# Fewer, wider VectorE operations for the router's choice, the slot's place and the attention's division

## The reference

```
x = x + attn_a(norm(x))    # delta-rule recurrence, 16 heads of 8, state 8x8 per head, gate, Wout
x = x + ffn(norm(x))       # 8 experts, top 2, capacity 640, weights w_g, c_fc, c_proj
x = x + attn_b(norm(x))    # linear attention: q' (k'^T v) / (q' . sum k'), then W_out, b_out
x = x + ffn(norm(x))       # the same experts again
```

```
top_v, top_i = top_k(logits, 2)
exp_rank = cumsum(one_hot(top_i) in the order (choice, token)) - 1
keep = exp_rank < cap
exp_out = gelu(batch @ c_fc) @ c_proj
```

## Time and profile before

| | |
|---|---|
| median of 3 runs | 482.74 us (482.45 to 485.15) |
| the profiled execution | 483.11 us |
| its span, first to last instruction | 481.4 us |
| busy: PE, DVE, ACT, POOL | 87%, 64%, 49%, 53% |
| granted TensorE clock, mean | 0.951 |
| DVE instructions | 744 |

### The profile page before, as it was taken

The page is one execution under the profiler, slowest core; times in us unless marked ns, Lnnn a source line. Parts: engine busy times, 40 slices in busy tenths (PEclk is TensorE's granted clock), DMA queues, the critical chain, the costliest instruction groups (busy, mean ns, idle before and its releaser), DMA issues.

```text
span 481.4 us, 8149 instructions
## 1 busy us (share of the span) xinstructions
PE 418.6 (87%) x2850; PEld 304.6 (63%) x2850; DVE 310.0 (64%) x744; ACT 236.5 (49%) x371; POOL 257.0 (53%) x321
## 2 busy tenths in 40 slices
PE   7889795878898899999898999889878979999970
PEld 6534352334697899999864333345347969999960
DVE  4898789999663323415696999899985602431364
ACT  4877755343230354343168988878762204435320
POOL 4899584899678865465305000020556732556470
PEclk9999899787899999999999999999997999999995
DMA  5457580993171232225624434595011121221276
GB/s 143 128 154 291 157 259 27 321 311 109 36 231 50 67 89 61 82 61 206 185 63 104 99 96 99 136 284 186 24 33 46 51 84 40 63 87 58 81 253 203
DMA packets 50328, 60.89 MB, mean 126 GB/s; under 512 B 7152, under 2 KB 29296, under 8 KB 50288
## 3 DMA queue, kind: packets, MB, share of 16 engines
q1 hardware_dynamic: 42672, 47.50, 33.4%
q0 software_dynamic: 4608, 8.47, 5.4%
q10 hardware_dynamic: 3008, 4.40, 2.8%
HBM read 29.78 MB, written 25.31 MB: 114 GB/s over the span
## 4 chain that ended last, share of the span: by engine, by line
PE 38%; DVE 11%; issue 9%; ACT 8%; DMA 6%; POOL 5%; ACTq 1%; POOLq 0%; DVEq 0%; SPq 0%
PE ps L1412 34%; DVE feat L1332 5%; POOL slots_x L517 4%; ACT expo L865 3%; PE ps L1568 2%; DMA xe<-slots_x 2%; DMA last_got<-chosen_y 2%; ACT rows_x L712 1%; DMA chosen_y<-ye,y_to 1%; DMA slots_x<-rows_x,put_at 1%; ACT xnT L610 1%; DVE stats L1064 1%; POOL chosen_y L567 1%; DVE part L1312 1%; DVE xres L1359 1%
## 5 line engine op out<-in xcount | busy, mean ns | idle before, releaser
L567 POOL DMA_INDIRECT chosen_y<-ye,y_to x80 | 79.1, 989 | 67.8 <-DVE ye L1277 49.4
L1332 DVE SCALAR_TENSOR_TENSOR feat<-expo,ps 128x1024 f32<-128x1024 f32 x64 | 75.1, 1214 | 6.3 <-ACT expo L865 6.2
L751 ACT ACTIVATE hT<-ps 128x640 f32<-128x640 f32 x64 | 45.2, 706 | 69.1 <-PE ps L1412 69.1
L517 POOL DMA_INDIRECT slots_x<-rows_x,put_at x64 | 62.8, 980 | 28.8 <-issue 17.7
L865 ACT ACTIVATE expo<-ps,minus_one 128x1024 f32<-128x1024 f32 x64 | 69.9, 1115 | 11.7 <-PE ps L1412 9.6
L1412 PE MATMUL ps<-cproj_sb,hT 128*128 128x128 f32 x640 | 74.6, 275 | 0.3
L1416 PE MATMUL ps<-ident 128*128 128x128 f32 x546 | 68.0, 285 | 7.5 <-DMA slots_x<-rows_x,put_at 4.1
L1412 PEld LDWEIGHTS ps<-cproj_sb,hT 128*128 128x128 f32 x640 | 72.9, 192 | 0.6 <-ACT hT L751 0.6
L1416 PEld LDWEIGHTS ps<-ident 128*128 128x128 f32 x546 | 63.9, 147 | 10.0 <-DMA slots_x<-rows_x,put_at 5.1
L1227 DVE TENSOR_TENSOR xe_low<-ps,xeT 128x640 fp32r<-128x640 f32 x16 | 13.2, 825 | 86.3 <-ACT xeT L610 86.3
L500 POOL TENSOR_TENSOR read<-state,qT 128x512 f32<-128x512 f32 x30 | 38.1, 1276 | 15.1 <-DVE state L1013 14.9
(11 more groups left out here) (238 smaller groups left out, 702.1 us busy)
## 6 DMA issues: line engine op xcount, KB each, us to landing
chosen_y<-empty_rows SPq DMA_DIRECT2D x32, 256.0 KB
decay<-k_rows SPq DMA_DIRECT2D x30, 256.0 KB, 5.1
stk<-part SPq DMA_DIRECT2D x96, 64.0 KB, 2.0
slots_x<-empty_rows SPq DMA_DIRECT2D x16, 325.0 KB, 6.1
xe<-slots_x SPq DMA_DIRECT2D x16, 325.0 KB, 2.9
cfc_sb<-in_L_ffn_c_fc SPq DMA_DIRECT2D x2, 2048.0 KB, 9.8
got<-chosen_y SPq DMA_DIRECT2D x8, 256.0 KB, 5.8
got<-chosen_y ACTq DMA_DIRECT2D x8, 256.0 KB, 7.0
```

What stands on the lines that cost most here:

```text
L517: pool.indirect_dma_start(out=slots_x[k], out_offset=bass.IndirectOffsetOnAxis(ap=put_at[:, c, kk, t:t + 1], axis=0), in_=rows_x[:, kk * N ...
L567: pool.indirect_dma_start(out=chosen_y[k], out_offset=bass.IndirectOffsetOnAxis(ap=y_to[:, b, i:i + 1], axis=0), in_=ye[:, b, i * D:(i + 1 ...
L751: act.activation(hT[:, b, f, :].rearrange("p (a n) -> p a n", a=2), ps[:, 2 + 2 * (f % 2):4 + 2 * (f % 2), 0:HALF], ACT.Gelu).then_inc(h_r ...
L1332: dve.scalar_tensor_tensor(out=feat[:, g % 4, :], in0=expo[:, g % 3, :], scalar=1.0, in1=flat(ps[:, pair, :]), op0=ALU.min, op1=ALU.max).t ...
```

## The change

Four things are done. In `choose` the test for a tie is made once for all four tiles into a new tile `tie`, ahead of `hit`, and one subtraction takes back the marks. In `locate` one product takes the place of two; for that the ranks are laid out by expert and then tile (`e t` where it was `t e`), in `rank` on TensorE too, and the reduction reads `table` with the tile innermost in its result. In `divide` one product takes the place of two; `att` gets the order (tile, g, gp, a, d) of its columns, so the columns of W_out are loaded in that order, by two transfers in place of one.

```diff
+        tie = sb("tie", [P, TB])
-        table = sb("table", [P, 4, TB, NE])
+        table = sb("table", [P, 4, NE, TB])
-            att = sb("att", [P, 2, TB, D], F32, b)
+            att = sb("att", [P, 2, TB, 4, 2, 2, HD], F32, b)
...
-            sp.dma_start(wnat[:, 3, :], W_out).then_inc(wnat_in, 16)
+            for n in range(2):
+                sp.dma_start(wnat[:, 3, :].rearrange("p (g n r) -> p g n r", g=4, n=2)[:, :, n, :],
+                             W_out[:, n * D // 2:(n + 1) * D // 2].rearrange("p (g r) -> p g r", g=4)).then_inc(wnat_in, 16)
...
                 link(ins)
+                steps[0] += 1
+                dve.tensor_tensor(tie[:], eight[:, :, 0], eight[:, :, 1], ALU.is_equal).then_inc(route_step, 1)
                 dve.tensor_tensor(hit, lg.unsqueeze(2).broadcast_to((P, TB, 2, NE)),
                                   eight[:, :, 0:2].unsqueeze(3).broadcast_to((P, TB, 2, NE)),
                                   ALU.is_equal).then_inc(logit_used, 1)
                 dve.wait_ge(logit_used, k * NB + c + 1)
-                for t in range(TB):
-                    ins = dve.scalar_tensor_tensor(out=hit[:, t, 1, 0:1], in0=eight[:, t, 0:1], scalar=eight[:, t, 1:2],
-                                                   in1=hit[:, t, 1, 0:1], op0=ALU.is_equal, op1=ALU.subtract, reverse1=True)
-                link(ins)
+                dve.wait_ge(route_step, steps[0])
+                link(dve.tensor_tensor(hit[:, :, 1, 0], hit[:, :, 1, 0], tie[:], ALU.subtract))
...
-                for kk in range(2):
-                    ins = dve.tensor_tensor(
-                        table[:, 2 * kk:2 * kk + 2, :, :], ranks[:, 2 * kk:2 * kk + 2, :, :],
-                        chosen[:, c, kk, :, :].rearrange("p e t -> p t e").unsqueeze(1).broadcast_to((P, 2, TB, NE)),
-                        ALU.mult)
-                ins.then_inc(rank_used, 1)
+                dve.tensor_tensor(table[:].rearrange("p (k n) e t -> p k n (e t)", k=2),
+                                  ranks.rearrange("p (k n) e t -> p k n (e t)", k=2),
+                                  chosen[:, c, :, :, :].rearrange("p k e t -> p k (e t)").unsqueeze(2)
+                                  .broadcast_to((P, 2, 2, NE * TB)), ALU.mult).then_inc(rank_used, 1)
                 dve.wait_ge(rank_used, k * NB + c + 1)
-                link(dve.tensor_reduce(place, table[:], AX_X, ALU.add))
+                link(dve.tensor_reduce(place, table[:].rearrange("p r e t -> p r t e"), AX_X, ALU.add))
...
-                for a_ in range(2):
-                    ins = dve.tensor_tensor(
-                        att[:, c % 2, :, gp * 64:(gp + 1) * 64].rearrange("p t (g a d) -> p t g a d", a=2, d=HD)[:, :, :, a_, :],
-                        rows.rearrange("p (t g) r -> p t g r", g=4)[:, :, :, 9 * a_:9 * a_ + HD],
-                        rden[:, gp, :, a_].rearrange("p (t g) -> p t g", g=4).unsqueeze(3).broadcast_to((P, TB, 4, HD)),
-                        ALU.mult)
-                ins.then_inc(att_ready, 1)
+                dve.tensor_tensor(att[:, c % 2, :, :, gp, :, :].rearrange("p t g a d -> p (t g) a d"),
+                                  pairs[:, :, :, 0:HD],
+                                  rden[:, gp, :, :].unsqueeze(3).broadcast_to((P, TB * 4, 2, HD)),
+                                  ALU.mult).then_inc(att_ready, 1)
...
-                ch = chosen[:, c, :, :, :].rearrange("p k e t -> p k t e")
-                up = upto[:, c, :, :, :].rearrange("p k e t -> p k t e")
-                twice = lambda ap: ap.unsqueeze(1).broadcast_to((P, 2, TB, NE))
+                ch = chosen[:, c, :, :, :]
+                up = upto[:, c, :, :, :]
+                twice = lambda ap: ap.unsqueeze(1).broadcast_to((P, 2, NE, TB))
...
-                    pe.wait_ge(wnat_in, 32)
+                    pe.wait_ge(wnat_in, 48)
```

More of the change, by code:

```diff
@@ L1177, in _ @@
                 if b is not None:
-                    locate(0, b, ps[:, 5 if b < NB - 1 else 4, P:2 * P].rearrange("p (r t e) -> p r t e", r=4, e=NE),
+                    locate(0, b, ps[:, 5 if b < NB - 1 else 4, P:2 * P].rearrange("p (r e t) -> p r e t", r=4, e=NE),
                            ps[:, 5, 3 * P:3 * P + 4 * TB].rearrange("p (r t) -> p r t", r=4))
@@ L1373, in _ @@
                 dve.tensor_copy(kvl[:, :, a_, :, cols], heads[:, :, a_, :, cols]).then_inc(kvl_ready, 1)
-            ranks_in = lambda bank: ps[:, bank, P:2 * P].rearrange("p (r t e) -> p r t e", r=4, e=NE)
+            ranks_in = lambda bank: ps[:, bank, P:2 * P].rearrange("p (r e t) -> p r e t", r=4, e=NE)
             for n in range(2, N_SLOT):
@@ L1537, in rank @@
             def rank(k, c, bank):
-                out = ps[:, bank, P:2 * P].rearrange("p (r t e) -> p r t e", r=4, e=NE)
-                ch = chosen[:, c, :, :, :].rearrange("p k e t -> p k t e")
-                up = upto[:, c, :, :, :].rearrange("p k e t -> p k t e")
-                twice = lambda ap: ap.unsqueeze(1).broadcast_to((P, 2, TB, NE))
+                out = ps[:, bank, P:2 * P].rearrange("p (r e t) -> p r e t", r=4, e=NE)
+                ch = chosen[:, c, :, :, :]
+                up = upto[:, c, :, :, :]
+                twice = lambda ap: ap.unsqueeze(1).broadcast_to((P, 2, NE, TB))
                 if k == 0 or c:
                     pe.wait_ge(chosen_ready, k * NB + c + (k == 0 and c < NB - 1))
-                mm(out, ones_bf[:], base_share[:].unsqueeze(2).broadcast_to((P, 4, TB, NE)), stop=False)
+                mm(out, ones_bf[:], base_share[:].unsqueeze(3).broadcast_to((P, 4, NE, TB)), stop=False)
                 for b in range(c):
                     first, second = (upto[:, b, kk, :, TB - 1] for kk in range(2))
-                    mm(out[:, 0:3, :, :], ones_bf[:], first.unsqueeze(1).unsqueeze(2).broadcast_to((P, 3, TB, NE)),
+                    mm(out[:, 0:3, :, :], ones_bf[:], first.unsqueeze(1).unsqueeze(3).broadcast_to((P, 3, NE, TB)),
                        start=False, stop=False)
-                    mm(out[:, 2, :, :], ones_bf[:], second.unsqueeze(1).broadcast_to((P, TB, NE)), start=False, stop=False)
-                    mm(out[:, 3, :, :], minus_bf[:], second.unsqueeze(1).broadcast_to((P, TB, NE)), start=False, stop=False)
+                    mm(out[:, 2, :, :], ones_bf[:], second.unsqueeze(2).broadcast_to((P, NE, TB)), start=False, stop=False)
+                    mm(out[:, 3, :, :], minus_bf[:], second.unsqueeze(2).broadcast_to((P, NE, TB)), start=False, stop=False)
                 pe.wait_ge(chosen_ready, k * NB + c + 1)
@@ L1553, in rank @@
                 mm(out[:, 2, :, :], ones_bf[:], up[:, 1, :, :], start=False, stop=False)
-                mm(out[:, 2, :, :], ones_bf[:], up[:, 0, TB - 1:TB, :].broadcast_to((P, TB, NE)), start=False, stop=False)
+                mm(out[:, 2, :, :], ones_bf[:], up[:, 0, :, TB - 1:TB].broadcast_to((P, NE, TB)), start=False, stop=False)
                 mm(out[:, 3, :, :], minus_bf[:], up[:, 1, :, :], start=False, stop=False)
@@ L1848, in turn_att @@
                 for t in range(TB):
-                    ins = pe.transpose(ps[:, bank, t * P:(t + 1) * P], att[:, c % 2, t, :], ident[:])
+                    ins = pe.transpose(ps[:, bank, t * P:(t + 1) * P], att[:, c % 2, t, :, :, :, :].rearrange("p g n a d -> p (g n a d)"), ident[:])
                 ins.then_inc(att_turned, 1)
```

## The result

| | before | after |
|---|---|---|
| median, 20 runs each, on one chip | 483.70 us (480.67 to 488.05) | 486.99 us (483.84 to 490.42, one at 540.02) |
| ratio to before, 95% interval | | 1.0072 (1.0044 to 1.0099) |
| the profiled execution, its span | 483.11, 481.4 us | 489.33, 487.5 us |
| DVE instructions, busy | 744, 310.0 us | 712, 311.6 us |

The kernel became 3.5 us slower by the ratio (0.72%; the medians differ by 3.3) where I forecast 0.1. The execution of 540.02 us had a granted clock of 0.73 and is left out of the ratio. The kernel has 32 VectorE instructions less, and VectorE is busy for longer.

The account below looks back on a forecast made before the run. VectorE's chain of waits, through TensorE and ScalarE, was taken to bound two stages ahead of the experts. First stage +0.29 and second -0.21 give +0.08 us on the profiled 483.11; from the median 482.74, forecast 482.8 us, range 480.4 to 485.4.

Parts of the forecast that it names:

- What bounds the kernel, and where the edits stand: VectorE's chain of waits in two stages ahead of the experts; each edit priced where it stands, block 3 worth nothing.
- The tie test in the first call: Choices of blocks 0 and 1: test held by one GpSimd product, each about 0.1 us slower; block 2 worth nothing.
- through two GpSimd products: Rival, chance 0.08: first-call tie test held through two adjoining products, each choice 1.2 us behind, +2.4 us, 485.2 us.
- The counter-row: Clamp at line 972 (23.34 us) ended inside six GpSimd products, 0.14 us after the second; used against the double hold.
- The tie test in the second call: Blocks 0 and 1: 0.39 us saved per choice, but line 1359's projection is next late, so 0.05 us gained each.
- The place: Eight calls: one table product saves 0.065 us, the stepped reduction costs 0.09; net +0.03 us each, six on the path.
- The division and W_out's load: One product (0.425 us) for two (0.49): -0.065 us each, three on the chain, -0.2; the two loads stay hidden.
- The second stage as a whole: 300 to 390 us: choices -0.1, divisions -0.2, places +0.09, together -0.21 us.
- The clock: Rival, chance 0.09 either way: TensorE's low-clock stretch near 112 to 121 us ends at once (480.2) or lasts (486.3).

Follow-up runs that it names:

- experiment 11: Changed kernel with four GpSimd fills of 128x512 ahead of block 0's reading product; 488.47 us, ratio 1.0087 to the kernel before.
- 12: Changed kernel with three GpSimd fills ahead of block 0's reading product; 487.59 us, ratio 1.0097 to the kernel before.
- experiment 13: Changed kernel with the first three scatters of each block's row one to three slots later; 485.26 us, ratio 1.0034 to the kernel before.
- experiment 2: Kernel before with the new tie correction alone; 487.25 us, ratio 1.0077 to the kernel before.
- experiment 5: Changed kernel with one tie-test operand and the last scan's reset pattern in PSUM in the first call; 483.30 us, ratio 0.9958 to the kernel before.
- 4: Changed kernel with the tie test moved behind the comparison; 485.87 us, ratio 1.0073 to the kernel before.
- 7: Changed kernel with four more MAX8 ahead of the real ones in the first call; 488.40 us, ratio 1.0087 to the kernel before.
- 8: Changed kernel with two more MAX8 ahead of the real ones in the first call; 488.25 us, ratio 1.0069 to the kernel before.
- experiment 14: Changed kernel with a 128x64 GpSimd fill behind each of the first two scatters of block 0's row; 489.45 us (four executions), ratio 1.0102 to before.
- experiment 10: Changed kernel with GpSimd's scatter put between the reading and decay products of a slot; 486.02 us, ratio 1.0040 to the kernel before.
- experiment 1: Changed kernel with the old tie correction of four operations; 482.82 us, ratio 1.0008 to the kernel before.
- experiment 3: Changed kernel with one operand of the tie test in PSUM in the first call; 483.51 us, ratio 0.9987 to the kernel before.

## Why the prediction was wrong

*What bounds the kernel, and where the edits stand:* right. The whole loss arose at the first call's choices of blocks 0 and 1, which I had named as the places where the wait moves.

*The tie test in the first call:* this step failed. I wrote "I take it to be held likewise: until 75.31 + 0.15 = 75.46, and 101.09 + 0.15 = 101.24", and so +0.1 for each block. Block 0 did this: its hold of 1.05 us is that of one product, and MAX8 to MAX8 grew by 0.27 with the place in it, where I had 0.13. At block 1 the test was held by two products. That is the mechanism of my rival "through two GpSimd products", to which I gave 0.08. It was even too cheap: I priced it at 1.2 us a block at two blocks, 485.2 us in all and inside my range, and it came at one block with 4.5 us. From MAX8 to the end of the last scan it was 3.03 us (99.44 to 102.47) and is 6.71 (101.58 to 108.29), +3.68, as the late test put the scan ahead of a second pair of products; the shift at line 1080 then added 0.79.

*The counter-row* I used against that rival, the clamp inside a row of six products at 23.34 us, was true but not like block 1. (By that product's own record, 22.92 to 24.20 us, it ended some 0.05 behind the second product and not 0.14.) Experiments 11, 12 and 13 show that where no scatter stands beside the products each wait is for one. The pair at block 1 stands between two scatters: before has one ahead of it too, from 98.58 to 99.79 us. I had looked at the two products and not at what GpSimd did ahead of them. In before nothing with two SBUF inputs is asked in the first product of that pair, so its rows there don't show the double hold; the last scan at 101.40 is asked in the second. That is why the trace of before could give the rival no more than a doubt, but I should have kept it in the range with its knock-on.

*The tie test in the second call:* right. The sum at line 1357 has a new idle time, of 0.24 us where I said 0.35:

```profile
337.04 0.17 DVE L1091 TENSOR_TENSOR tie<-eight 128x4 f32<-128x4 f32 x1
...
340.04 0.69 DVE L1357 TENSOR_TENSOR xres<-ps,xres 128x512 f32<-128x512 f32 x1 [0.24 <-PE ps L1410]
```

From MAX8 (336.61) to that sum it is 3.43 us, before 3.47: 0.04 gained, forecast 0.05. At the second place (MAX8 at 353.29) it is 3.43 and was 3.46. There the sum has no new idle time; VectorE stood for 0.32 us ahead of the subtraction at line 1097 instead, behind the comparison, which no other choice of this trace shows and the same choice of experiment 2 doesn't either. Why is open.

*The place:* right. The table product took 284 ns (forecast 285), the stepped reduction 388 where the unstepped one took about 290: +0.10, forecast +0.09. The estimate by the Trainium skill's "Vector Engine (DVE) Microarchitecture Reference", section "Measured stream behaviour on trn2", was +0.09 to +0.19; the row lies at its lower end.

*The division and W_out's load:* right. 425 ns as forecast; the two issues take 0.49 and 0.51 us, and TensorE's transposes of these weights come at 45.6 us, 38 us later.

*The second stage as a whole:* from its first MAX8 to the last scatter 58.22 us before, 58.19 after; forecast -0.21. Right in sign and too small to tell.

*The clock:* its phase differs between executions by more than the range I gave. The runs of before spread from 480.67 to 488.05, so a range of 5 us around one profiled execution was too narrow, even with the steps right.

## What to carry to other kernels

Count the operands in SBUF before the instructions: beside GpSimd products that read SBUF, a VectorE operation of four elements with two SBUF inputs cost up to 2.5 us here and then pushed the next one into the same wait, while four small operations with one input in PSUM cost 0.6. Where such an operation must stand there, give it one PSUM operand (0.16 us in the same place), and look at the next one with two: in experiment 5 the hold went on to the difference at line 1115. When an operation is made to wait, follow everything of its kind behind it, and read the other engine's timeline one instruction further back than the one that runs.

## What the runs showed of the hardware

- Two holds of different length. An operation of VectorE with two SBUF inputs that is asked for beside GpSimd's two-tensor products ends 0.02 to 0.16 us behind one of them. Without a scatter beside the products it is let in after the running one (1.05 us at block 0 of after, 1.22 in experiment 11, 1.05 and 1.18 in experiment 13). When asked just ahead of or in the first of two adjoining products with a scatter on both sides, it waits for both: 2.22 to 2.59 us for the tie test in after and in experiments 2, 4, 7, 8, 11, 12 and 14, 2.77 to 2.87 for the scan in these and in experiment 10. Asked in the second, it waits for that one (the last scan of block 1: 1.07 us before, 1.08 in experiment 1, 1.25 in experiment 3). A fill of 0.17 us between the scatter ahead and the pair doesn't alter this (experiment 14); taking the scatters on both sides away does (experiment 13).
- Why a scatter should do this, and whether it is the one ahead of the pair or the one behind it, stays open. No run has a test or scan asked in the first product of a pair with a scatter on one side only, none used another kind of DMA on GpSimd, and the shift at line 1080 shows only single holds.
- One SBUF input was enough for the clamp at line 972: in before it took 0.90 us at 23.34, beside GpSimd's two-tensor products, and 0.18 at 20.27, beside none of them. The reciprocal behind it, also with one, took 0.55 at both places. So the count of SBUF inputs isn't the whole rule.
- The Trainium skill, "SBUF — State Buffer", section "SBUF: two separate sides", says that of VectorE and GpSimd whichever starts first has the shared port pair for the whole instruction. The single holds and the PSUM operands agree (0.16 us in experiment 3). The double holds go beyond what it states, and the scan at 105.52 us in after was in the records 0.13 us ahead of the product at 105.65 and still waited for it.
